# A graph network layer pair on one core: edge chunks gathered in one fixed stream, and a single overflow pass

## What is computed

```python
def _block(x, edge_index, edge_weight, g, bln, W, b):
    h = _layer_norm(x, g, bln)
    # GCN: self-loops, deg = segment_sum(ew, dst), norm = dis[row] * ew * dis[col]
    h = segment_sum((h @ W.T)[row] * norm[:, None], col) + b
    return x + relu(h)
```

## Time and profile before

| | us |
|---|---|
| median of 3 runs (6287.8 to 6318.42) | 6317.9 |
| span of the profiled execution | 4375.4 |
| the profiled execution's own time | not recorded apart from its span |
| TensorE busy / VectorE / ScalarE / GpSimd | 3602.6 / 2502.6 / 1195.2 / 3096.7 |
| mean granted TensorE clock | 0.914 of full |
| stage one, to the first gather | 253.0 |
| first gather of layer 1 to first gather of layer 2 | 2036.6 |
| first gather of layer 2 to the end of the span | 2085.8 |

### The profile page before, as it was taken

One profiled execution on the slowest core, in us unless ns is written; L12 is line 12 of the kernel. 1 busy time (PEld: TensorE's weight loads), 2 busy tenths in 40 slices (PEclk: granted clock), 3 DMA queues, 4 the chain that ended last, 5 costly groups with the idle time before them and its releaser, 6 DMA issues.

```text
span 4375.4 us, 93734 instructions
## 1 busy us (share of the span) xinstructions
PE 3602.6 (82%) x26676; PEld 3057.6 (70%) x26677; DVE 2502.6 (57%) x8948; ACT 1195.2 (27%) x3161; POOL 3096.7 (71%) x3340
## 2 busy tenths in 40 slices
PE   5976766766776776767778999999999999999989
PEld 4855655655655655655657888888888887888878
DVE  8854555554554554544555665665666565665655
ACT  2520100100110110101113444444444444444434
POOL 3357777777777777777767777777777777777772
PEclk9988888888888888888889999999999999999999
DMA  4144444444444444444433343443344343343331
GB/s 150 50 139 119 129 126 124 129 126 119 131 129 119 130 130 119 130 123 126 127 111 116 112 117 115 115 118 115 112 117 118 111 117 115 115 118 115 115 111 53
DMA packets 256046, 515.38 MB, mean 118 GB/s; under 512 B 61480, under 2 KB 154032, under 8 KB 255984
## 3 DMA queue, kind: packets, MB, share of 16 engines
q0 software_dynamic: 151392, 413.60, 33.2%
q1 hardware_dynamic: 104592, 101.17, 6.9%
HBM read 474.81 MB, written 39.71 MB: 118 GB/s over the span
## 4 chain that ended last, share of the span: by engine, by line
PE 48%; DVE 14%; issue 12%; POOL 11%; DMA 7%; ACT 4%; DVEq 2%; SPq 1%; POOLq 0%; ACTq 0%
PE bank L1282 46%; POOL gs L521 11%; DMA gr<-h_d,idx_r 7%; DVE ss L1038 2%; PE bank L1304 2%; ACT L696 1%; DVE rstd L717 1%; DVE rstd L715 1%; DVE rstd L716 1%; DVE st L724 1%; ACT bank L696 1%; DVEq L269 1%; DVE w L1179 1%; ACT w L699 1%; DVEq L1038 1%
## 5 line engine op out<-in xcount | busy, mean ns | idle before, releaser
L521 POOL DMA_INDIRECT gs<-h_d,idx_all x3038 | 2902.3, 955 | 957.5 <-issue 659.4
L1282 PE MATMUL bank<-gs,ss 128*128 128x256 f32 x6272 | 1601.5, 402 | 12.3 <-DMA gs<-h_d,idx_all 12.3
L1282 PEld LDWEIGHTS bank<-gs,ss 128*128 128x128 f32 x6272 | 1219.9, 202 | 191.7 <-DMA gs<-h_d,idx_all 23.2
L1038 DVE TENSOR_SCALAR ss<-iw,dst_all,ew 128x128 f32<-128x128 f32 x3152 | 882.9, 354 | 183.8 <-PE bank L1282 125.8
L696 ACT ACTIVATE bank<-bank,eb1c 128x128 f32<-128x128 f32 x1616 | 448.8, 340 | 634.3 <-PE bank L1282 633.8
L1282 PE MATMUL bank<-experts,w 128*128 128x256 f16 x4848 | 605.3, 278 | 16.8 <-DVE w L1179 16.8
L1282 PE MATMUL bank<-w,experts 128*128 128x128 f16 x9696 | 608.4, 220 | 0.0
L1282 PEld LDWEIGHTS bank<-w,experts 128*128 128x128 f16 x9696 | 569.0, 98 | 44.4 <-issue 16.6
L1282 PEld LDWEIGHTS bank<-experts,w 128*128 128x128 f16 x4848 | 468.4, 100 | 91.1 <-issue 22.1
L1282 PE MATMUL bank<-gr,sr 128*128 128x256 f32 x232 | 115.6, 593 | 479.2 <-DMA gr<-h_d,idx_r 479.2
L1179 DVE SCALAR_TENSOR_TENSOR w<-bank,w 128x512 f16<-128x512 f32 x404 | 278.3, 689 | 360.9 <-ACT w L699 360.4
(11 more groups left out here) (270 smaller groups left out, 3434.1 us busy)
## 6 DMA issues: line engine op xcount, KB each, us to landing
gs<-h_d,idx_all POOLq DMA_INDIRECT x3038, 2.7
hself<-h_d SPq DMA_DIRECT2D x100, 128.0 KB, 3.2
ew_in<-in_eW SPq DMA_DIRECT2D x49, 168.0 KB, 2.6
out<-u SPq DMA_DIRECT2D x51, 128.0 KB
u<-xn_d SPq DMA_DIRECT2D x50, 128.0 KB, 3.4
h_d<-u SPq DMA_DIRECT2D x50, 128.0 KB, 1.9
u<-x_d SPq DMA_DIRECT2D x50, 128.0 KB
u<-r_d SPq DMA_DIRECT2D x50, 128.0 KB, 2.8
```

Of the source, the lines that this page charges most:

```text
L521: pool.indirect_dma_start(gs[:, n, :], None, table[:, :], bass.IndirectOffsetOnAxis(ap=idx_all[:, w, n:n + 1], axis=0), element_offset=P * ...
L1038: m = dve.tensor_scalar(ss[:, slot + j, :], iw[:, :], dst_f[:, bass.ds(c, 1)], ew[:, bass.ds(c, 1)], ALU.is_equal, ALU.mult)
L1282: return pe.matmul(out_ap, lhsT, rhs, start=first, stop=last, **kw)
```

## The change

Chunk c of a layer is gathered once, into slot c mod 32 of `gs`, in the order 0 to 1562. The index is read straight from `src_row`, so the index list that VectorE made in stage one goes. Block w always uses the 36 chunks 32w - 2 to 32w + 33 (the last block 29), two at each border being shared with its neighbours' spans through their slots; the table lookups of T_LO and T_SHARED in the layers go. Scatter tiles are in nine groups of four in a ring of 18.

The rest loops go. Chunks of a block outside its fixed span are counted by two prefix sums over blocks (left and right of the span, 98 segments), and one loop per layer handles them ahead of the first block (`over`), at least one step: VectorE finds segment, chunk and block, GpSimd gathers the rows after its fourth regular gather, TensorE multiplies, VectorE adds the product to the block's row tile, and SP loads and stores that row tile. As this changes self-loop rows, they come from tables of their own, `self1_d` and `self2_d`, into which SP stores the same tiles as into `h1_d` and `h2_d`.

```diff
-STATIC = U * PIECES
-OWN = STATIC - 1
-SLOTS = OWN
-S_SLOTS = 16
-EARLY = (8, 16)
+OWN = U * PIECES - 1
+CH = 32
+SIDE = 2
+USES = CH + 2 * SIDE
+GROUPS = USES // U
+LAST_CH = NCH - CH * (W - 1)
+LAST_USES = LAST_CH + SIDE
+SLOTS = CH
+S_SLOTS = 18
+BEFORE_OVER = 4
 LO_MIN = 1
...
+SEGS = 2 * W
+OVER_MAX = SEGS * NCOL
+OVER_LINKS = 10
+OVER_BLOCK, OVER_INDEX, OVER_SPREAD, OVER_SUM = 5, 7, 9, 10
...
+        self1_d = nc.dram_tensor("self1_d", [(W + 2) * P, D], F32).ap()
+        self2_d = nc.dram_tensor("self2_d", [(W + 2) * P, D], F32).ap()
...
-        idx_all = sb("idx_all", [P, W, OWN], I32); idx_r = sb("idx_r", [P, 1], I32)
-        gs = sb("gs", [P, SLOTS, D]); gr = sb("gr", [P, D])
-        ss = sb("ss", [P, S_SLOTS, P]); sr = sb("sr", [P, P])
-        iw = sb("iw", [P, P]); iw_rest = sb("iw_rest", [P, P])
+        idx_o = sb("idx_o", [P, 1], I32)
+        gs = sb("gs", [P, SLOTS, D]); go = sb("go", [P, D])
+        ss = sb("ss", [P, S_SLOTS, P]); so = sb("so", [P, P])
+        iw = sb("iw", [P, P]); iw_o = sb("iw_o", [P, P])
+        over_old = sb("over_old", [P, D]); over_new = sb("over_new", [P, D])
...
+        def over_step(layer, base, t, step):
+            return (base + t) * OVER_LINKS + (layer + 1 + step)
+        def chunk_turn(layer, w, n):
+            return layer * (W if n < LAST_CH else W - 1) + w
...
-            def h1_rows(g):
-                sp.dma_start(h1_d[(g * XG + 1) * P:((g + 1) * XG + 1) * P, :].rearrange("(t p) d -> p t d", p=P),
-                             xh[:, g * XG:(g + 1) * XG, :]).then_inc(s["h1_out"], 16)
+            def h1_rows(t, n):
+                for table, done in ((h1_d, s["h1_out"]), (self1_d, s["self1_out"])):
+                    sp.dma_start(table[(t + 1) * P:(t + n + 1) * P, :].rearrange("(t p) d -> p t d", p=P),
+                                 xh[:, t:t + n, :]).then_inc(done, 16)
...
+            def over(layer, table):
+                n = over_count(sp)
+                base = layer * n
+                with sp.Fori(0, n, 1) as t:
+                    sp.wait_ge(s["over_links"], over_step(layer, base, t, OVER_BLOCK))
+                    sp.sem_inc(s["gate"], 1)
+                    r0 = sp.snap(sp.value_load(over_cell[0:1, CELL_BLOCK:CELL_BLOCK + 1], min_val=0, max_val=W) * P + P)
+                    sp.dma_start(over_old[:, :], table[bass.ds(r0, P), :]).then_inc(s["over_old"], 16)
+                    sp.wait_ge(s["over_links"], over_step(layer, base, t, OVER_SUM))
+                    sp.dma_start(table[bass.ds(r0, P), :], over_new[:, :]).then_inc(s["over_out"], 16)
+                    sp.wait_ge(s["over_out"], (base + t) * 16 + 16)
+                    sp.sem_inc(s["gate"], 1)
+            sp.wait_ge(s["self1_out"], 16 * (W // XG + 1))
+            over(0, self1_d)
+            sp.dma_start(hself[:, :], rows(self1_d, 1)).then_inc(s["self_in"], 16)
...
                 sp.dma_start(h2_d[bass.ds(here, P), :], u4[:, :]).then_inc(s["h2_out"], 16)
+                sp.dma_start(self2_d[bass.ds(here, P), :], u4[:, :]).then_inc(s["h2_out"], 16)
...
+            over(1, self2_d)
...
+            def over(layer, table):
+                n = over_count(pool)
+                base = layer * n
+                with pool.Fori(0, n, 1) as t:
+                    pool.wait_ge(s["over_links"], over_step(layer, base, t, OVER_INDEX))
+                    pool.sem_inc(s["gate"], 1)
+                    pool.indirect_dma_start(
+                        go[:, :], None, table[:, :],
+                        bass.IndirectOffsetOnAxis(ap=idx_o[:, 0:1], axis=0), element_offset=P * D).then_inc(s["over_in"], 16)
             def gathers(layer, table):
                 pool.wait_ge(s[f"table{layer + 1}"], 1)
-                def chunks(w, some):
...
+                for c in range(NCH):
+                    g, n = layer * W + c // CH, c % CH
+                    if n >= CH - SIDE:
+                        pool.wait_ge(s["main_used"], g * USES + (n - (CH - SIDE)) + 1 + S_SLOTS)
+                    elif g:
+                        pool.wait_ge(s["main_used"], (g - 1) * USES + n + SIDE + 1 + S_SLOTS)
+                    pool.indirect_dma_start(
+                        gs[:, n, :], None, table[:, :],
+                        bass.IndirectOffsetOnAxis(ap=src_row[:, c:c + 1], axis=0),
+                        element_offset=P * D).then_inc(s[f"main_in{n}"], 16)
+                    if c == BEFORE_OVER - 1:
+                        over(layer, table)
+            pool.wait_ge(s["tab_set"], OVER_TABLES)
...
+            dve.tensor_scalar(lo, last, float(1 - OWN), float(LO_MIN), ALU.add, ALU.max)
+            dve.scalar_tensor_tensor(out=left, in0=own_at, scalar=float(-SIDE - 1), in1=last, op0=ALU.add, op1=ALU.min)
+            ch.link(dve.scalar_tensor_tensor(out=start_r, in0=own_at, scalar=float(CH + SIDE), in1=first, op0=ALU.add,
+                                             op1=ALU.max))
+            dve.tensor_tensor(n_deg, lo, first, ALU.subtract)
+            dve.scalar_tensor_tensor(out=left, in0=left, scalar=1.0, in1=first, op0=ALU.add, op1=ALU.subtract)
+            ch.link(dve.scalar_tensor_tensor(out=right, in0=last, scalar=1.0, in1=start_r, op0=ALU.add, op1=ALU.subtract))
+            dve.tensor_scalar(n_deg, n_deg, float(OWN - DEG), 1.0, ALU.add, ALU.max)
+            dve.tensor_scalar(n_left, left, 0.0, None, ALU.max)
+            ch.link(dve.tensor_scalar(n_right, right, 0.0, None, ALU.max))
...
-            def index_list(t, lo):
-                dve.tensor_copy(idx_all[:, bass.ds(t, 1), :].rearrange("p a c -> p (a c)"),
-                                src_row[:, bass.ds(lo, OWN)]).then_inc(s["idx_listed"], 1)
...
+            def over(layer):
+                n = over_count(dve)
+                base = layer * n
+                links = s["over_links"]
+                step, seg, high = (over_at[:, i:i + 1] for i in (AT_STEP, AT_SEG, AT_HIGH))
+                dve.memset(step, 0.0).then_inc(links, 1)
+                with dve.Fori(0, n, 1) as t:
+                    def done(i):
+                        return over_step(layer, base, t, i)
+                    dve.wait_ge(links, done(0))
+                    dve.tensor_scalar(over_le[:, :], over_cum[:, :], step, None, ALU.is_le).then_inc(links, 1)
+                    dve.wait_ge(links, done(1))
+                    dve.tensor_scalar(step, step, 1.0, None, ALU.add).then_inc(links, 1)
+                    dve.tensor_reduce(seg, over_le[:, :], AX.X, ALU.add).then_inc(links, 1)
+                    dve.wait_ge(links, done(3))
+                    dve.tensor_scalar(high, seg, float(W), float(-W), ALU.is_ge, ALU.mult).then_inc(links, 1)
+                    dve.wait_ge(links, done(4))
+                    dve.tensor_tensor(over_cell[:, CELL_BLOCK:CELL_BLOCK + 1], seg, high, ALU.add).then_inc(links, 1)
+                    dve.tensor_copy(over_cell[:, CELL_SEG:CELL_SEG + 1], seg).then_inc(links, 1)
+                    dve.wait_ge(links, done(6))
+                    dve.sem_inc(s["gate"], 1)
+                    at = dve.value_load(over_cell[0:1, CELL_SEG:CELL_SEG + 1], min_val=0, max_val=SEGS)
+                    off = dve.value_load(over_tab[0:1, bass.ds(at, 1)], min_val=0, max_val=2 * OVER_MAX)
+                    c = nc.s_assert_within(dve.snap(off + t - OVER_MAX), 0, NO_EDGES)
+                    w = dve.value_load(over_cell[0:1, CELL_BLOCK:CELL_BLOCK + 1], min_val=0, max_val=W)
+                    dve.tensor_copy(idx_o[:, :], src_row[:, bass.ds(c, 1)]).then_inc(links, 1)
+                    dve.tensor_scalar(iw_o[:, :], iota_p[:, :], win_first[:, bass.ds(w, 1)], None, ALU.add).then_inc(links, 1)
+                    dve.wait_ge(links, done(8))
+                    dve.tensor_scalar(so[:, :], iw_o[:, :], dst_f[:, bass.ds(c, 1)], ew[:, bass.ds(c, 1)],
+                                      ALU.is_equal, ALU.mult).then_inc(links, 1)
+                    dve.wait_ge(s["over_used"], base + t + 1)
+                    dve.wait_ge(s["over_old"], (base + t) * 16 + 16)
+                    dve.tensor_tensor(over_new[:, :], wide(4), over_old[:, :], ALU.add).then_inc(links, 1)
+            def scatter_group(v, k, at, uses=USES):
+                if k * U >= uses:
+                    return
                 dve.wait_ge(s["main_used"], v + k * U + U)
-                slot = k * U % S_SLOTS
...
+                for u in range(k * U, min(k * U + U, uses)):
+                    c = bass.ds(at + (FRONT + u - SIDE), 1)
+                    m = dve.tensor_scalar(ss[:, u % S_SLOTS, :], iw[:, :], dst_all[:, c], ew_all[:, c], ALU.is_equal, ALU.mult)
+                m.then_inc(s["main_set"], U if k * U + U < uses else USES - k * U)
...
+            over(0)
...
-                dve.wait_ge(s["rest_used"], lo + off + 1)
+                dve.wait_ge(s["main_used"], v + USES + S_SLOTS)
...
+            over(1)
...
-            def messages(turn, v, k, fresh=False):
...
+            def messages(layer, w, k, uses=USES):
```

(30 more changed lines are left out.)

268 lines of the change are left out of this document (94 added, 174 removed).

## The result

The change took 5194.8 us (median of four runs, 5192.4 to 5201.1) beside 6308.6 us before (four runs, 6287.8 to 6318.4): ratio 0.824, 95% interval 0.8216 to 0.8265, 1114 us less. The forecast was 6225, the range 6178 to 6290. The sign was right, the size twelve times too small (93 us forecast).

What follows compares the result with a forecast made beforehand. GpSimd issuing one gather per 1.25 us was taken as the bound, TensorE close behind. Terms +10 - 48.8 + 0.5 - 53.4 - 1.7 = -93.4 us took 6317.9 to 6225 us; range 6178 to 6290 with rivals.

Steps and rivals of the forecast that it cites:

- Rival 4: Time around the span shrinks in proportion, or unprofiled gathers are slower: gain 135 us, time 6183 us; chance 10%.
- The stall of a rest step: GpSimd waits for VectorE's index at a block's second rest step: 3.6 us beyond usual, 18 times; layer 1's nine 32.4 us.
- start of layer 1: SP storing layer 1's rows to two tables on one queue delays the first gather: +10 us, bounds 0 and +17.
- layer 1's gathers: Nine rest stalls and 13 gathers fewer in layer 1, at 1.262 us spacing: -48.8 us.
- change of layers: Between the layers, one more 128 KB store before table 2 is released: +0.5 us.
- layer 2 to block 47's last gather: Layer 2's gathers up to block 47's last chunk: 1942 us against 1995.6, -53.4 us, overflow stall included.
- from there to the end: After block 47, TensorE sets the time and block 48 has 29 products, not 33: -1.7 us.
- overflow stall of layer 2: After four gathers of layer 2, GpSimd waits for VectorE's overflow index: +8.3 us, bounds +6 and +15.
- TensorE's pace: TensorE's own time per block in layer 2 rises from 38.6 to 39.9 us, just under the gathers' 40.3.
- rival 1: TensorE becomes the bound of layer 2, at 40.7 us a block: 6253 us, or 6267 at 41; chance 17%.
- Rivals 2, 3 and 5: 2: TensorE waits for scatter tiles, 6357 us, 5%; 3: more tiles delay gathers, 6262, 4%; 5: several overflow steps, 6315, 4%.
- The rule against it: Trainium skill: VectorE in a 2-port mode shuts GpSimd out of shared ports, so more scatter tiles would slow gathers.

Runs made afterwards that it cites:

- a_same: The changed kernel, unchanged, timed again on a slow chip: 5143.7 us against 6240.3 for the kernel before, ratio 0.8241.
- b_rest_l1_4: The kernel before with rest steps in layer 1 only (layer 2's 58 left out), on a slow chip: 5655.2 us against 6251.7, ratio 0.9048.
- a_same_2: The changed kernel, unchanged, timed again on a quick chip: 4293.1 us against 4378.5 for the kernel before, ratio 0.9806.
- a_no_over: The changed kernel without the overflow pass on all engines, in both layers, on a slow chip: 5145.2 us.

## Why the prediction was wrong, point by point

**The step that failed** is "what lies around it is taken as the median's 6317.9 - 4375.4 = 1942.5 us and carried over unchanged". 1.7 us lie around the span. The 1942 us are inside the span of the runs that were timed (6229.5 of 6231.2 us in the job of a_same), and a profile of a run that was 1942 us shorter was taken for them. So every term that is a wait had a price from the wrong chip. Rival 4, that the time around the span goes with the change, had the direction and 10%, but as a proportion (a gain of 135 us); what went was one kind of wait.

**The stall of a rest step**, 3.6 us for 18 of 116, is the term that carries the miss. On the slow kind layer 2's 58 steps cost 596 us, 10.3 each, where the prediction had 9 stalls of 3.6 us and the steps' own issue. What the change does beyond leaving these out is read trace against trace, from b_rest_l1_4 to a_same, whose timeline at the start and end of layer 1 and the start of layer 2 is:

```profile
260.76 1.30 POOL L571 DMA_INDIRECT gs<-h_d,src_row  x1 [28.31 <-SPq L379]
...
2596.05 0.95 POOL L571 DMA_INDIRECT gs<-h_d,src_row  x1 [1.87 <-remote]
2641.29 0.95 POOL L571 DMA_INDIRECT gs<-h_d,src_row  x1 [44.30 <-SPq L423]
```

Layer 1, which loses its rest steps and gains products, goes from 2939.6 to 2335.3 us, 604 less. The first gather comes 8.6 us later, the change of layers takes 45.2 instead of 14.1 us, and layer 2, with its further gathers and products, 2501.6 instead of 2444.7. Together 8.6 - 604.3 + 31.1 + 56.9 - 596.4 = -1104 us, where 1097 and 1114 were measured. The two traces are of different slow chips (the kernel before at 6252 and 6240 us), so this holds to some 10 us, an estimate; and that layer 1's 604 us are its rest steps is concluded from layer 2, where they were left out by themselves.

**The other terms were near**, on the chip they were worked out for: 10 us off in the sum, with one 14 us off. Span against span, and the timeline above:

| term | forecast | quick chip |
|---|---|---|
| start of layer 1 | +10 | 260.98 - 253.03 = +7.9 |
| layer 1's gathers | -48.8 | 1987.31 - 2021.75 = -34.4 |
| change of layers | +0.5 | 16.13 - 14.86 = +1.3 |
| layer 2 to block 47's last gather | -53.4 | 1938.15 - 1995.55 = -57.4 |
| from there to the end | -1.7 | 89.5 - 90.2 = -0.7 |
| sum | -93.4 | -83.3 |

Layer 1's spacing is 1.271 us where 1.262 was taken. The issue of a gather got longer: 966 ns in the mean in layer 1 where it was 956, over 1564 gathers 16 us, where the term is 14 off. The added time stands beside VectorE's operations on two full SBUF tiles, as here (a_same_2):

```profile
1041.17 1.25 POOL L571 DMA_INDIRECT gs<-h_d,src_row  x1 [0.30 <-issue]
1041.19 0.42 DVE L1168 SCALAR_TENSOR_TENSOR u<-t_b,xn_keep 128x256 f32<-128x256 f32 x1
```

In layer 1 the 227 gathers that overlap such an operation take 1070 ns in the mean, where 243 took 998 before; those that overlap a scatter tile and none of them take 952 (957 before), all others 947 (945). It is a coincidence in time, not an experiment. The overflow stall of layer 2 was put at 8.3 us and is 8.84 from gather to gather (2268.16 to 2277.00), 7.6 beyond the usual spacing. TensorE's pace was put at 39.9 and is 39.8 alone; in the changed kernel it is busy 794.5 of 800 us in layer 2 (3000 to 3800) and hidden by a hair, so rival 1 did not decide. Rivals 2, 3 and 5 are out: TensorE keeps its 39.8 us, a gather takes 959 ns and no more beside scatter tiles than before, and there is one overflow gather a layer. Two slips in the numbers decide nothing: the bounds of the forecast's own range add to 6193 to 6259, not 6200 to 6255, and the trace of before has 3152 scatter tiles, not 3168, so rival 3's price is 148 x 0.28 = 41 us.

**The rule against it.** A gather is 943 ns at the least and 949 in the median in the changed kernel's first trace, on a slow chip, and 941 and 947 on a quick one, with 3514 scatter tiles for 3152: for scatter tiles, nothing of shared ports is to be seen, as in the earlier trace rows. For operations on two full tiles it is otherwise, as the means above show; the median hides them.

**What the profile can't show.** Late signals show as idle time in front of the one that waits, 17.7 us after a product of 1.05 us has ended. By the Trainium skill (Perfetto Trace Analysis, Summary: the profiler window per engine type) an instruction's record ends before its semaphore update has travelled. By that rule the way of a signal stands in no engine's busy time. The traces agree: on both kinds of chip the changed kernel's VectorE is busy 2503 to 2524 us and its GpSimd 3073 to 3081.

**The sign that was overlooked** stood in the table ahead of the prediction: a profiled execution with a span 1942 us short of the time. Nothing in a launch of one core was known to last that long. The forecast should have held two cases, one of them that the timed runs are made of waits that the profile doesn't show, and then a change that takes out 116 round trips between three engines has a far larger reach than 93 us.

## What to carry to other kernels

If span and time disagree, the profile is not one of the runs that are timed; settle that before any term is summed, and give the cases in which waits are dearer a price of their own. A loop in which a queue waits for an index that another engine writes late in its program is cheap only as long as signals are quick: on a slow chip each turn cost 10.3 us instead of 2.0. A fixed stream with its order known ahead costs three more products a block and has no such turn; it is still 20% slower on the slow kind, by the other late signals.

## What was not expected of the hardware

Two chips run one program 43% apart (6240 against 4377 us) with VectorE and GpSimd equally busy in the changed kernel, and the mean granted clock is lower where the waits are (0.801 and 0.915; 0.75 in layer 1 of b_rest_l1_4 for 0.85 on a quick chip). On the slow kind, signals are late where gathers are issued at 1.25 us each: by 14.8 to 19.1 us in the first block of four traces, 20 to 34 us after the first gather, where in a_no_over VectorE was in time 8 us after it, and by 3.2 us in the median in front of ScalarE in layer 2; with half of the gathers that is 0.8 us, and both kinds are within 1.5%. VectorE's waits on itself went from 0.19 to 1.41 us in places of one trace only. On either kind, the issue of a gather is longer beside a VectorE operation on two full tiles (in layer 1, 1070 ns for 947 on the quick kind, 1028 for 945 on the slow one). Whether the slow kind is the chip or what surrounds it, and whether recording the events has a part in it, stays open.
